# Cross attention of the second layer: the value sums of a block issued as one run, ahead of the steps beside them

## What is computed

```python
q = jnp.einsum('bsc,hcd->bhsd', xn, wq)
k = jnp.einsum('btc,hcd->bhtd', yn, wk)
v = jnp.einsum('btc,hcd->bhtd', yn, wv)
a = jax.nn.softmax(jnp.einsum('bhsd,bhtd->bhst', q, k) * D ** (-0.5), axis=-1)
...
o = jnp.einsum('bhst,bhtd->bhsd', a, v)
```

## Time and profile before

| | |
|---|---|
| median of 3 runs | 4335.58 us (4334.79 to 4337.01) |
| the profiled execution, its own time | 4342.75 us |
| its span, first to last instruction | 4341.5 us |
| mean granted TensorE clock | 0.881 |
| PE busy | 3683.3 us, 85% |
| DVE, ACT, POOL busy | 52%, 38%, 22% |
| the stage `a2` in that span | about 2555 to 3602 us |

### The profile page before, as it was taken

One profiled execution on the slowest core, in us unless ns is written; L12 is line 12 of the kernel. 1 busy time (PEld: TensorE's weight loads), 2 busy tenths in 40 slices (PEclk: granted clock), 3 DMA queues, 4 the chain that ended last, 5 costly groups with the idle time before them and its releaser, 6 DMA issues. The chain is left out here.

```text
span 4341.5 us, 58736 instructions
## 1 busy us (share of the span) xinstructions
PE 3683.3 (85%) x22060; PEld 2148.6 (49%) x22060; DVE 2258.0 (52%) x4083; ACT 1657.7 (38%) x3025; POOL 967.5 (22%) x1022
## 2 busy tenths in 40 slices
PE   6679999999997973778876489999999995799998
PEld 4433444444433842444545344555555544576767
DVE  6647567566671344544424356666676533333332
ACT  1125546555464220233334124545555453222222
POOL 1100000000000011233333214554545452200000
PEclk9857979889896985788988768999999997899999
DMA  1111211212111302343321142433434411121211
GB/s 35 34 45 44 58 37 45 52 40 64 36 45 59 108 6 62 52 72 60 58 48 37 48 68 44 63 59 55 61 54 60 61 18 62 55 68 58 63 59 59
DMA packets 144194, 229.41 MB, mean 53 GB/s; under 512 B 40868, under 2 KB 90792, under 8 KB 140840
## 3 DMA queue, kind: packets, MB, share of 16 engines
q1 hardware_dynamic: 143912, 225.65, 24.7%
HBM read 99.39 MB, written 8.91 MB: 25 GB/s over the span
## 5 line engine op out<-in xcount | busy, mean ns | idle before, releaser
L893 DVE TENSOR_REDUCE a_mp<-bank 128x1 f32<-128x384 f32 (+2 forms) x1280 | 704.6, 592 | 470.7 <-PE bank L751 463.3
L859 ACT ACTIVATE a_p<-bank 128x512 f32<-128x512 f32 (+1 forms) x1088 | 593.8, 596 | 690.5 <-PE bank L776 670.3
L859 ACT ACTIVATE mx_p<-bank 128x512 f32<-128x512 f32 (+3 forms) x1088 | 549.1, 557 | 500.6 <-PE bank L776 282.8
L893 DVE TENSOR_REDUCE mx_mp<-bank 128x2 f32<-128x768 f32 (+4 forms) x640 | 598.3, 957 | 272.7 <-PE bank L751 164.9
L929 POOL TENSOR_TENSOR a_pair<-a_p 128x512 f32<-128x512 f32 x384 | 487.8, 1303 | 522.9 <-ACT a_p L859 522.7
L751 PE MATMUL bank<-a_ks,a_qs 96*128 96x384 f32 (+2 forms) x1280 | 451.4, 424 | 80.5 <-issue 59.3
L776 PE MATMUL bank<-a_qs,a_ks 98*128 98x512 f32 (+1 forms) x1088 | 430.6, 463 | 40.1 <-DMA a_qs<-a_mt 24.5
L751 PEld LDWEIGHTS bank<-a_ks,a_qs 96*128 96x128 f32 x1280 | 259.2, 204 | 238.4 <-issue 139.4
L200 POOL TENSOR_TENSOR rs<-ve,neghalf 128x4 f32<-128x4 f32 (+2 forms) x80 | 77.7, 972 | 1341.9 <-DVE ve L195 1305.1
L776 PE MATMUL bank<-mx_qs,mx_ks 50*128 50x512 f32 (+3 forms) x1088 | 352.3, 505 | 20.9 <-DMA mx_qs<-mx_mt 13.0
L751 PE MATMUL bank<-mx_ks,mx_qs 48*128 48x384 f32 (+4 forms) x1280 | 324.8, 449 | 11.8 <-issue 7.4
(11 more groups left out here) (293 smaller groups left out, 5557.7 us busy)
## 6 DMA issues: line engine op xcount, KB each, us to landing
sf_raw<-in_h_w SPq DMA_DIRECT2D x64, 512.0 KB, 3.5
a_ks<-a_kh SPq DMA_DIRECT2D x96, 192.0 KB, 4.5
ex_w<-in_L_ffn_w SPq DMA_DIRECT2D x16, 1024.0 KB, 4.9
a_qs<-a_qh SPq DMA_DIRECT2D x64, 256.0 KB, 6.0
mx_ks<-mx_kh SPq DMA_DIRECT2D x192, 48.0 KB, 2.1
a_ks<-a_kl SPq DMA_DIRECT2D x48, 192.0 KB, 5.2
mx_qs<-mx_qh SPq DMA_DIRECT2D x128, 64.0 KB, 2.2
mx_rec<-mx_flat SPq DMA_DIRECT2D x128, 64.0 KB, 2.0
```

Of the source, the lines that this page charges most:

```text
L859: act.activation(probs[place % len(probs)][0:kp, q0:T], self.bank(part, n, kb, h)[0:kp, q0:T], ACT.Exp, scale=scale).then_inc(*self.frees( ...
L893: v.tensor_reduce(best[:, tiled * j:tiled * j + tiled, i, ci], bank[:, 0:w] if tiled == 1 else bank[:, :, 0:w], AX.X, ALU.max).then_inc(*s ...
```

## The change

In `a2`, no value sums stand in a block's first half. In its second half, both parts of the block before are written, part 0 then part 1, after the first peaks and ahead of the steps beside. The other stages keep their order.

```diff
@@ -614,7 +614,9 @@
             for part in range(2):
 
                 sums = [("values", *blocks[at - 2 + part], 1 - part)] if at > 1 - part else []
-                if job.summed and part == 0:
+                if job.pairs:
+                    sums = [("values", *blocks[at - 1], i) for i in range(2)] if part and at else []
+                elif job.summed and part == 0:
                     yield from sums
                 yield "weigh", n, kb, part
                 if job.pairs and kb | 1 < last and kb % 2:
@@ -644,7 +646,8 @@
                 yield from beside_half()
                 yield from peaks(to, most - (found - was))
         for block, part in ((-2, 1), (-1, 0), (-1, 1)):
-            yield "values", *blocks[block], part
+            if block == -1 or not jobs[0].pairs:
+                yield "values", *blocks[block], part
```

## The result

Six executions of the changed kernel have a median of 4311.46 us (4300.17 to 4320.62), six of the kernel before 4338.68 (4334.79 to 4349.98). The ratio is 0.9931, with a 95% interval of 0.9913 to 0.9949: 22 to 38 us faster. The change was run twice more beside the kernel before, with ratios of 0.9919 (0.9896 to 0.9942) and 0.9905 (0.9882 to 0.9928). The forecast was 34 us, a ratio of 0.9922.

A forecast was written before the change was run, and what follows sets the result against it. PE was taken to bound a2; 119 fewer runs of 32-column matmuls at 0.32 us save 38 us, less 4 for ACT, so 34 us: 4301.6 us off the median of 4335.58, range 4288 to 4324.

The forecast's parts named there:

- PE bounds a2, and a run leaves no gap: In a2, PE busy 239 to 250 of 260 us per stretch; what leaves its list without a gap is won.
- 0.32 us a run: Each run of 32-column matmuls removed from a2 saves 0.08 going in, 0.14 itself and going out, 0.10 at first scores.
- 38 us less 4: In a2, 119 fewer runs of 32-column matmuls save 38 us; ACT loses 4, leaving 34 us.
- the term of 4 us for ACT at V o V: Where a product stood between two value parts, 21 places, ACT's copy delays exponentials by up to 0.2 us each.
- The moved part waits for nothing, the buffers don't matter: Part 1 needs the same exponentials as part 0, so adds no wait; ACT's buffers freed half a block sooner count nothing.
- POOL: Pair sums have 0.4 us in hand before ACT's exponentials; nothing taken, wrong if ACT's waits for them pass 40 us.
- What I said would show it: Value and score loads idle for "issue" about 120 times fewer, 16-record value rows 1.07 us, a2 ending about 34 us earlier.
- V W V: Values, sum of weights, values between second-half and next scores; with a following values part, 51 places, one run before and after.
- that the saved time is swallowed: Rival: scores' wait for ACT grows by what PE saves; 4330 us, 0 to 8.7 us off; chance 0.06.
- that a part costs as much in a long run: Rival: adjacent value parts still cost 0.57 us each, so nothing is saved; 4335 us; chance 0.02.
- that peaks run into DVE to the point of a loss: Rival: PE waits a 0.63 us reduce at 97 places, 61 us less 38 won; 4359 us; chance 0.04.
- that more than 48 us are won: Rival: waits in the way of the removed runs go with them; 4280 us; chance 0.05.

The follow-up runs named there:

- half: The change for every second block only, part 1 of the others staying at the next block's head; 4321.2 us, ratio 0.9950 to the kernel before.
- late: Against the kernel before, both parts and any sum of weights in one run, buffers freed as late as before; 4311.28 us, ratio 0.9927.
- apart: The change with part 0 directly behind the second half's scores, ahead of the peaks, so the parts don't touch; 4337.82 us, 0.9998 to the kernel before.
- spread: The change with one peak instead of two ahead of the value sums in a block's second half; 4294.04 us, ratio 0.9889 to the kernel before.

## Why the prediction was right

- **PE bounds a2, and a run leaves no gap**: right. The stretches became shorter with the same work in them, and half and the change follow the number of runs: 64 and 119 runs fewer gave 22 and 37 us. `late` doesn't follow it to the end: 128 fewer gave 30.
- **0.32 us a run**: 0.34 in the one place compared, 0.34 and 0.31 a run over the stage in half and in the change, and 0.32 to 0.34 at the full clock for a block with one run less (the change, half) or more (apart). The pieces, as medians of start to start over the trace before at the full clock: two peaks of 450 columns hold PE 0.50 us ahead of values and 0.41 ahead of a product (0.09, forecast 0.08). Values alone hold it 0.57 us, and in the change both parts in one run 1.00, so that the second adds 0.43 (0.14, as forecast). Two scores hold it 0.57 us behind values and 0.47 behind a peak (0.10, as forecast).
- **The pieces beside a product**: off in opposite ways at the place shown. The product gave back 0.17 us, not 0.08, and the first scores after it 0.03, not 0.10, since they hold PE 0.54 us and not the 0.47 forecast. That the sum fits there too is in part luck.
- **38 us less 4**: measured 36.8 at the same clock, 30, 35 and 41 us by the ratios. Whether the term of 4 us for ACT at V o V is there is not shown: scores wait for ACT 1, 2 and 5 us longer than the 79.1 before in the three profiles. The peaks' waits for DVE, which I had taken at nothing with a bound of 10 us, rose by 17. `spread` shows that such waits take the place of others, so the 17 us are not 17 us lost.
- **The moved part waits for nothing, the buffers don't matter**: nearly. `apart` has the earlier release and no gain, `late` the gain without the release, but 7 us less of it.
- **POOL**: ACT's waits for it rose from 17.3 to 24.9 us, far under the 40 that I named.
- **What I said would show it**: score loads idle 115 times for the 100 forecast. Value loads fell by 220, not by about 120: the idle entries also count the turn from the sum of weights back to values inside one run, which went with V W V. The count of such entries is not the count of runs; I used it only to find the place. In the trace before, values hold PE 0.46 us when sums of weights follow, which have 32 columns too, and 0.57 us when anything of full width follows; sums of weights hold it 0.86 us ahead of values and 0.97 ahead of full width (medians at the full clock). So it is the change of width that costs, not the change from one kind of matmul to another.
- **Wrong in the text, without effect on the sum**: the clock. I treated it as a constant of the stretches and put its spread nowhere but in the upper bound. It moves a single execution by up to 18 us either way, as much as half the gain, and in `apart` it gave back what 58 runs cost.

The rivals: that the saved time is swallowed, that a part costs as much in a long run (the second part adds 0.43 us, not 0.57), that peaks run into DVE to the point of a loss, and that more than 48 us are won are all ruled out.

The page TensorEngine Tiling (Array Packing) of the Trainium skill, section Tiling Modes, says that a change of mode drains the engine and a change of tile does not. The trace agrees as to where time is lost, at each change between 128 and 32 output columns and not between values and sums of weights of one width, and the runs give the size that the page leaves out: 0.31 us for going in and out once. That this time is spent draining the engine, no run here shows.

## What to carry to other kernels

Where matmuls with few output columns alternate with full ones on a PE that bounds the stage, count how often PE's list changes from one kind to the other, price one change there and back from start to start in the timeline, and gather the small ones as far as their buffers allow. Before asking whether an earlier or a later place matters, build the kernel with the places and without the touching: it separates the two in one run. Compare kernels at the same granted clock when the effect is under 1%. The mean clock of each execution is enough as long as the clocks differ little; where one kernel keeps its clock in one stage, as `apart` did, compare the traces block by block where both are at the full clock. And let the window of a view of waits end where the stage ends: one that stopped at 3560 us showed 68.6 us of waits of scores for ACT in `apart`, and the whole stage has 79.6.

## What was not expected

- The mean granted clock differed between executions of one kernel run together by 0.012, 33 and 35 us in time, and over the whole program each microsecond at the lower level cost 0.296 us, not the 0.5 that a kernel bound by matmuls alone would lose.
- With more runs (`apart`) PE was at the lower level for only 13.7 us of a2, where all others profiled had 41 to 72 us (from 2580 us on). PE's idle time and its order differ there; which of them does it stays open.
